# Transformer tower on one core: VectorE splits the next unit's patches between the sum of the exponentials and its reciprocal

## The reference, cut to what matters

```python
h = _ln(relu(x @ ew1 + eb1) @ ew2 + eb2, eg, ebeta)
q, k, v = split(h @ aiw + aib, 3)                     # 16 heads of 16 features
attn = softmax(einsum('bhqd,bhkd->bhqk', q, k) * SCALE, axis=-1)
o = einsum('bhqk,bhkd->bhqd', attn, v)                # then h = o @ aow + aob, two LSTMs, gates, decoder
```

## Time and profile before

| | |
|---|---|
| median of three runs | 3985.1 us |
| the profiled execution | 3987.37 us |
| its span in the profile | 3985.4 us |
| TensorE busy (matmul) | 3549.4 us, 89% |
| VectorE busy | 2747.6 us, 69% |
| ScalarE busy | 2115.4 us, 53% |
| GpSimd busy | 1256.6 us, 32% |
| mean granted clock | 0.959 of full speed |
| L860 waiting for scores (L747) | 73.6 us of idle VectorE |
| GpSimd L665 waiting for L873 in the experts | 220.6 us, 252 times |

### The profile page before, as it was taken

One profiled execution on the slowest core, in us unless ns is written; L12 is line 12 of the kernel. 1 busy time (PEld: TensorE's weight loads), 2 busy tenths in 40 slices (PEclk: granted clock), 3 DMA queues, 4 the chain that ended last, 5 costly groups with the idle time before them and its releaser, 6 DMA issues. The chain is left out here.

```text
span 3985.4 us, 94491 instructions
## 1 busy us (share of the span) xinstructions
PE 3549.4 (89%) x35332; PEld 2154.8 (54%) x35332; DVE 2747.6 (69%) x4811; ACT 2115.4 (53%) x4188; POOL 1256.6 (32%) x1056
## 2 busy tenths in 40 slices
PE   6768778878878888899999999999999949999997
PEld 5644355555545545435555555555555537666665
DVE  7866688788688688766666666666666654555555
ACT  6857357657657657654444444444444455555554
POOL 0026467567567567520000000000000004444443
PEclk8989899989999999999999999999999969999999
DMA  9920100100100110231111111111111131111211
GB/s 175 176 53 17 43 16 0 44 16 0 44 16 1 44 65 1 86 122 45 50 45 50 45 50 45 50 45 50 45 50 45 45 113 51 56 43 54 56 56 31
DMA packets 391037, 203.23 MB, mean 51 GB/s; under 512 B 150861, under 2 KB 385106, under 8 KB 390234
## 3 DMA queue, kind: packets, MB, share of 16 engines
q1 hardware_dynamic: 390482, 201.03, 20.1%
q10 hardware_dynamic: 392, 0.03, 0.0%
HBM read 143.48 MB, written 57.51 MB: 50 GB/s over the span
## 5 line engine op out<-in xcount | busy, mean ns | idle before, releaser
L201 POOL MEMSET h_ident<- 128x128 f32 x1 | 0.2, 205 | 1444.2 <-POOLq L81 1444.2
L1866 ACT ACTIVATE l_gates<-l_gates 128x768 f32<-128x768 f32 x260 | 219.1, 843 | 349.4 <-DVE l_gates L1810 349.4
L1810 DVE SCALAR_TENSOR_TENSOR l_gates<-banks,l_unscale,l_bias 128x1024 f32<-128x1024 f32 x260 | 333.7, 1283 | 97.0 <-PE banks L1636 95.3
L665 POOL TENSOR_TENSOR ax_p<-ax_p,ax_ri 128x520 f32<-128x520 f32 (+1 forms) x256 | 320.2, 1252 | 220.6 <-DVE ax_ri L873 220.6
L1636 PE MATMUL banks<-l_w,l_xs 128*64 128x512 f16 x3120 | 361.9, 382 | 7.5 <-DVE l_xs L1723 6.6
L1636 PE MATMUL banks<-plot,l_xs 128*64 128x512 f16 x3120 | 359.9, 380 | 0.0
L2163 PE MATMUL banks<-h_mem,h_w 128*128 128x320 f16 x2496 | 357.6, 300 | 0.0
L1636 PE MATMUL banks<-l_w,out_t 128*64 128x512 f16 x3072 | 352.9, 379 | 1.7 <-DVE out_t L1729 1.7
L1636 PE MATMUL banks<-plot,out_t 128*64 128x512 f16 x3072 | 352.8, 379 | 0.0
L2458 ACT ACTIVATE h_work<-banks,h_bias,h_factor 128x320 f32<-128x320 f32 x312 | 192.4, 617 | 260.7 <-PE banks L2163 256.9
L1870 ACT ACTIVATE l_ig<-l_kept 128x256 f32<-128x256 f32 x260 | 108.2, 416 | 357.2 <-DVE l_kept L1827 355.3
(11 more groups left out here) (385 smaller groups left out, 7321.5 us busy)
## 6 DMA issues: line engine op xcount, KB each, us to landing
out_t<-x_scratch SPq DMA_DIRECT2D x130, 256.0 KB, 3.0
mem_scratch<-out_t SPq DMA_DIRECT2D x520, 64.0 KB, 2.0
h_mem<-mem_scratch SPq DMA_DIRECT2D x104, 320.0 KB, 3.6
image<-in_x_dram SPq DMA_DIRECT2D x132, 196.0 KB
x_scratch<-plot SPq DMA_DIRECT2D x4, 4160.0 KB, 16.3
ring<-in_x_dram SPq DMA_DIRECT2D x60, 196.0 KB
plot<-in_L_ffn_attn_in_w_dram SPq DMA_DIRECT2D x4, 768.0 KB, 4.6
h_scratch<-plot SPq DMA_DIRECT2D x1, 2080.0 KB, 6.5
```

Source lines behind the costliest of these rows:

```text
L665: pool.tensor_tensor(self.p[:, v, :, 0:k], self.p[:, v, :, 0:k], self.ri[:, v, :, 0:k].unsqueeze(3).broadcast_to([P, 2, k, SEQ]), ALU.mult ...
L1810: dve.scalar_tensor_tensor(out=gz.rearrange("p (n c) -> p n c", n=2), in0=ps[:, 2 * z:2 * z + 2, :], scalar=unscale[:, e:e + 1], in1=bias[ ...
L1866: act.activation(gates[:, z, 0:3 * D], gates[:, z, 0:3 * D], ACT.Sigmoid).then_inc(gated, 1)
```

## The change

In `dve_run`, the call of `dve_split` at s=0 is put between the sum (L871) and the reciprocal (L873). The reciprocal's condition, the same as that of the sum, is written out again. The instructions, their operands and the waits in front of each stay the same; only their order in VectorE's queue at s=0 changes.

```diff
                     dve.tensor_reduce(self.sm[:, v, :, 0:k], self.p[:, v, :, 0:k], AX.X, ALU.add).then_inc(self.summed, 1)
+                if s == 0 and self.unit_in(u, 1):
+                    self.dve_split(dve, src, unit + 1, at + 1, 1 - par, self.count(unit, u, 0))
+                if self.image_in(u, s, 1):
                     dve.wait_ge(self.summed, BASE + n(0))
                     dve.reciprocal(self.ri[:, v, :, 0:k], self.sm[:, v, :, 0:k]).then_inc(self.inverted, 1)
-                if s == 0 and self.unit_in(u, 1):
-                    self.dve_split(dve, src, unit + 1, at + 1, 1 - par, self.count(unit, u, 0))
                 if s == 2 and self.unit_in(u, 2):
                     self.dve_move(dve, src, unit + 2, at + 2)
```

## The result

The changed kernel takes 3971.85 us in the median of 11 runs (3968.01 to 3979.03), against 3985.1 us of 11 runs before (3981.84 to 3994.17): ratio 0.9963, 95% interval 0.9955 to 0.9971. The forecast was 3974.0, range 3966 to 3990. The profiled span went from 3985.4 to 3970.8 us. VectorE is busy 2689.0 us and not 2747.6, GpSimd 1217.2 and not 1256.6, with the same instructions. Most of it are single instructions that ran shorter: 56 x 0.74 = 41 us of L829 on VectorE, and 56 x (0.44 + 0.17) = 34 us of L636 and L665 on GpSimd.

The account below looks back on a forecast made before the run. Bound: a loop of VectorE up to the split's end, then TensorE from keys to next scores. Experts 56 x 0.18 = 10.1 us plus 1.0 in the first attention, 11.1 off 3985.1: 3974.0 us, range 3966 to 3990.

Parts of the forecast that it names:

- The wait for the split goes, and a wait for the masked keys comes in its place: TensorE's values of s=2, experts: 0.66 us of waiting for masked keys replaces the split wait, leaving 0.18 us gain.
- the 0.84 us that `x_low` gains: Experts' s=2 could start 0.84 us earlier if the mask were no gate; that rival had 47 us, 3938, 4%.
- The steps of the chain: Experts, from the sum through split, reciprocal, multiplication and mask to TensorE's values of s=2: 4.07 us, gaining 0.18.
- The split gets shorter, 0.69: L829 on VectorE takes 0.69 us, not 1.43, because GpSimd is idle during the split in the new order.
- "split stays long" rival: L829 keeps its 1.43 us, so s=2 starts 0.56 us later than before: 4016 us; chance 9%.
- 1.10 and not 1.28 for the signal: L636's start to L701 at s=2 takes 1.10 us; at 1.28 the experts gain nothing, about 3984, chance 20%.
- Is it kept?: Whether s=2's 0.18 us survives s=3: its mask lets L701 go at 558.76, TensorE arrives at 558.93, fitting by 0.17.
- A free semaphore: Rival between L871 and the split: L827 starts at 0.72 us, not 0.60, gain 0.06 per unit; 3981, chance 5%.
- The first attention: The six units there that share the reordering: -1 us taken in total, between bounds of +1.7 and -1.5.
- Both bounds: First attention, per unit: +0.29 us from a later s=2, -0.25 from an earlier reciprocal of image 0 helping s=3.
- the shorter signal: First attention: with a shorter signal from mask to values, s=2 starts 0.12 us later instead of 0.29.
- TensorE has no slack: First attention: the mask L636 for s=2 (318.96, 1.22 us) is used at 320.45, leaving TensorE no slack.

Follow-up runs that it names:

- early masks: GpSimd masks image 2's keys at s=0, ahead of the multiplication by the reciprocals: 3939.5 us in the changed kernel, 3990.3 us in the kernel before.
- Held with the old order: Kernel before, reciprocal still ahead of the split, with GpSimd's multiplication at s=0 also waiting for x_low: 3983.8 us, ratio 0.9991.
- the low half twice: Changed kernel with the low half of the split computed twice, first into a spare tile: 4014.4 us, ratio 1.0073.

## Why the prediction was right

*What bounds, and what takes its place.* "The wait for the split goes, and a wait for the masked keys comes in its place": shown by the after trace, and by the pair of early masks, which give 32 us or more in the changed kernel and nothing in the old one. Had I taken the 0.84 us that `x_low` gains for the gain of the unit, the forecast would have been 47 us instead of 11.

*The steps of the chain.* L871 to L827: 0.60 predicted, 0.60 measured. L827 to L829: 0.46, 0.45. To the reciprocal: 0.61, 0.61. To L665: 0.28, 0.27. To L636: 1.02, 1.02. To L701: 1.10, 1.09. The sum 4.07 became 4.04, the gain 0.18 became 0.21, a hundredth in each of three steps, and 10.1 us became 11.7. With the first attention that is 11.1 predicted and 13.3 measured, both in the stages and between the medians.

*The split gets shorter, 0.69.* Right in 60 of 64. What it is worth was not said apart in the prediction. Held with the old order it is worth 0.02 us a unit, because it is then paid back in the mask. In the new order the 0.74 us are on the chain. That is argued, from the run with the low half twice: 0.61 us more ahead of the reciprocal made s=2 start 0.60 later, so a long L829 would have made the "split stays long" rival come true.

*1.10 and not 1.28 for the signal.* That choice was the one between gain and none. It came from 12 cases at the same steps and not from the more numerous ones at s=1, where the wait is followed by two more in the stream. All 56 units at s=2 now show 0.05 to 0.06 us between the mask's end and the values; at s=1 it is still 0.23 to 0.24.

*Is it kept?* s=3 starts 3.42 us after s=2 (554.64 to 558.06), as predicted, without a wait for its mask, which GpSimd ended at 557.84.

*A free semaphore.* The Trainium skill (VectorE: DVE Perf Modes, "The DRAIN you can't avoid") says of eight copies in a row that the semaphore costs nothing extra; carried over to this place, that would have put L827 0.72 us after L871. It started 0.60 after it, 0.08 before its end, so it does not carry over to this pair, and the rival is out. The first paragraph of the same section says that an instruction that is not held starts earlier, and with that the trace agrees.

*The first attention.* -1.0 predicted between +1.7 and -1.5; -1.6 measured, just past the better end. Both bounds came true, each at its own step, and the -1 between them was a guess. TensorE before (the unit whose L871 starts at 316.86), and after (318.79):

```profile
319.42 1.10 PE L987 MATMUL banks<-a_x,a_cols 128*128 128x512 f32 x2 [0.71 <-DVE a_x L1023]
...
324.07 0.46 PE L995 MATMUL banks<-a_cols,a_x 128*64 128x64 f32 x8 [0.56 <-issue]
```

```profile
322.49 0.46 PE L996 MATMUL banks<-a_cols,a_x 128*64 128x64 f32 x8 [0.80 <-issue]
...
325.74 0.46 PE L996 MATMUL banks<-a_cols,a_x 128*64 128x64 f32 x8 [0.19 <-issue]
```

The values of s=2 start 3.70 us after the sum instead of 3.59, as the shorter signal had it, those of s=3 6.95 instead of 7.21, and the unit takes 13.21 us instead of 13.46: 6 x 0.25 = 1.5 us. One reading was not right: "TensorE has no slack" there. The first bracket says that it waited 0.71 us for the split. The mask of s=2 ended 0.27 us before its use, and where the values do wait for it, after the change, they start 0.10 us behind its end, so the mask had some 0.17 us to spare. That is why the early mask gave nothing in the old order.

## What to carry to other kernels

When a wait of the bounding engine is removed, follow each thing that was moved later until it meets the same engine again; here the gain was set by the second wait (0.21 of 0.84 us), and one more reordering, of an instruction with no part in the change, released three times as much of the unit (0.65 us). An instruction's duration in a profile belongs to its place: look who runs beside it before it is moved. And a reordering is worth only what the present bound lets through, so the same edit was worth 0 and 32 us.

## What the runs showed of the hardware

*Of L829 and a GpSimd instruction beside it, the one that starts first is not slowed by the other, and the other is held.* L829 reads two tensors in SBUF. Started 0.35 us after L665 it took 1.43 us, started 0.15 us before it 0.69, and then L665 took 1.46 instead of 1.06; alone each takes 0.69 and 1.06. The Trainium skill (SBUF — State Buffer, "SBUF: two separate sides") says just this of a vector operation with two SBUF inputs beside a GpSimd operation that reads SBUF: the first has the shared port for the whole instruction. The traces agree on who is held, and the delay is a little less than what was left of the other instruction: L829 0.74 us where L665 had 0.88 left (552.79 to 553.67), L636 0.44 where L829 had 0.59 left (553.63 to 554.22), L665 0.40 where L829 had 0.54. L827 does it too, though it reads one tensor: in the kernel before, L665 starts 0.32 us ahead of L827's end and takes 1.23 us and not 1.06, in all 56 units. L860 and L865, whose large input is in PSUM, and the sums (L871) left GpSimd's 1.06 and 1.04 us alone.

*TensorE's clock at the start of an attention.* Between units 0 and 1 some executions lose 2 us in an expert. In the second expert of the kernel before, the keys that TensorE projects in unit 0 took 2.74 us:

```profile
831.63 2.74 PE L679 MATMUL banks<-ax_x,w_in 128*128 128x256 f16 x12 [1.40 <-DVE ax_x L829]
```

In the first expert of the changed kernel the same instructions took 1.49:

```profile
526.66 1.49 PE L679 MATMUL banks<-ax_x,w_in 128*128 128x256 f16 x12 [1.68 <-DVE ax_x L829]
```

The table by stretch (us, busy of each engine and instructions, granted clock, share of DMA, GB/s) says why: from 831 to 835 the first had 0.50, which is 1.2 GHz; from 526 to 530 the second had 1.00, 2.4 GHz.

```profile
831.00:835.00 4.00, 3.37 (x24) 2.25 (x24) 2.83 (x5) 1.79 (x4) 1.02 (x1) 0.50 0.02 4
```

```profile
526.00:530.00 4.00, 3.15 (x38) 2.22 (x39) 3.57 (x7) 2.53 (x6) 0.99 (x1) 1.00 0.02 4
```

Ahead of it TensorE had waited for the split in both, 1.40 and 1.68 us by the brackets. In the kernel with the low half twice the clock was low during these keys in all four experts (2.12 to 2.74 us), which by the steps from unit 0 to unit 1 is some 4 of the 7 us that its time lay above the expected; in the others it was low in none to four, in one each of the kernel before and the changed one. What decides between the two was not tried, so an effect of a few microseconds in a change of this kind can come from there alone.
